# A two-layer latent model on one core: cross attentions that loop over two tiles, shorter prologues, and core attention's weights made during the experts

## The chip, the cores and the metric

One core of a Trainium2 chip. The metric is the device time of one execution in microseconds (us), lower is better. TensorE (PE) has two clock levels, 1.2 and 2.4 GHz; the profile gives the granted clock as a share of the higher one.

## The reference, cut to what matters

64 batches of 32 rows with 256 columns go through two layers of three parts each, and each part adds its result to X (residual):

```
x0  cross attention, 16 heads of 128, 4 key groups, context 64 x 257 x 256 (layer 0)
a0  attention over 512 learned keys and values
e0  router, top 2 of 8 experts, plus one shared expert (inter 128)
c1  "core" attention over the rows themselves: LN, quantised to 8-bit floats per
    linear, heads layer-normed, softmax over 32 rows
x1  cross attention as above with 8 key groups, LN and quantisation (layer 1)
a1  difference attention, f1 feed-forward with Walsh-Hadamard rotations
```

In x0 and x1 a query is projected from the normed row, normalised per head and scored against 257 keys:

```
q = norm(LN(x) Wq) ;  k = norm(ctx Wk) ;  p = softmax(q k^T / sqrt(128))
x = x + (p (ctx Wv)) Wo
```

In c1 and x1 the heads are layer-normed, so the kernel subtracts from the weights of each head their mean over its 128 columns ("centring") before it projects, and in c1 it splits each weight into an upper part in a rounded matmul format and the rest, so that two fast matmuls stand for one exact one; Wo is split into three bf16 parts.

## The kernel before

X is held in SBUF as 16 tiles of 128 rows (four batches of 32). The parts run one after the other, each in a block of its own with its own semaphores, and each engine's program is written out by hand as one stream in order; there is no planner. Between parts GpSimd clears the semaphores.

**Cross attention** (`cross_attention`, both layers; names with `x_` in the rows). `run` (L271) calls `tile(i, cur, prev, nxt)` on each of PE, ACT, DVE and GpSimd: tile 0, then a hardware loop `Fori(1, 15)` of one tile per iteration (its branch instructions are L276 in the rows), then tile 15 and the rest of tile 15's output. SP has such a loop too. A tile has four slots, one for each batch. In a slot PE projects keys from the context (L383), sums squares (L391), scores (L402), transposes probabilities (L412), weighs the context with them (L420) and applies Wv (L429); at its place in the last slots the output Wo (L449) of the tile before, and the query of the tile after: LN'd rows `x_xn` transposed (L358), projected with `x_wq` (L367), transposed back per head (L374). LN of tile i+1 is made on DVE and ACT during tile i: `token_stats` (DVE L803, L806) and `rsqrt_tokens` (ACT L590, L593) at the start of slot 0, the norm itself `x_xn` (DVE L811) somewhat later in slot 0, and PE's L358 waits for it. `copy_weighed` (DVE L919) copies out the weighed context, `round_heads` (DVE L962) quantises in x1. The context of each batch, both ways round, is loaded by SP while the batch before is worked on.

**What stands ahead of the loops.** For x0 the program first has a block in which SP loads all of X (2 MB, L2843) and the identity (L2844) and waits for both; only then does x0's block begin, with SP issuing `x_wq` (2 MB, L288), `x_wk`, the small weights (norm weights, key bias, query bias of 1 MB, mask) and then contexts. PE and DVE wait for the small weights, DVE makes constants (L798, L799), then LN of tile 0, then the query of tile 0 (L367), then keys. In x1 DVE first centres all of `x_wq` (sum L786, subtract L788) and `x_wk`, makes constants (L789 to L795), and only then makes LN of tile 0 (L803 on).

**Experts** (`experts`, names `e_`): 4 passes of four tiles (512 rows as matmul columns). A pass transposes the normed rows (PE L1166), has the router (PE L1522) and its choice on DVE (L1597 to L1617), and nine expert steps: hidden A and B (L1530), gate on DVE (L1623), output Y (L1542), adds to X on DVE (L1586; the ninth, L1588). LN of the next pass (DVE L1141, L1146, L1151, ACT L1159) stands after the last gate. ACT, DVE and PE loop over passes 0 to 2.

**Core attention** (`core_attention`, names `c_`): its prologue loads constants, the three groups of weights and, when their buffer is free, the two halves of Wo; DVE makes 10 constants one after the other, LN of tile 0, centres the head weights (L2143, L2146, L2150), and with ACT splits head weights (L1977, L2154), values (L1934, L1937, L2158) and Wo (L1943, L1945, L2164, L2166). PE transposes tile 0 (L1783), waits for the split head weights before its first projection (L1797), and after the projections of tile 0 waits for the last part of Wo (`late`).

Of the kernel before, what the change touches and what calls it, by code (L numbers as in the profile page):

```python
# [16 lines left out]
P = 128  # L17
# [80 lines left out]
def cross_attention(nc, d, X, Yc, ident, layer, tiles):  # L98
# [25 lines left out]
    with Part(nc) as ctx:  # L124
# [18 lines left out]
        if L1:  # L143
            vecs = sb("vecs", [P, 24])
            inv_in = sb("inv_in", [P, HC])
            smooth = sb("smooth", [P, NH])
            inv_sm = sb("inv_sm", [P, NH])
            qbias = sb("qbias", [P, 1])
            wmean = sb("wmean", [P, HC, NH])
            yscale = sb("yscale", [P, 1])  # L150
# [51 lines left out]
        weights = ctx.semaphore(n + "weights")  # L202
        key_weights = ctx.semaphore(n + "key_weights")
# [83 lines left out]
        def _(sp):  # L287
            sp.dma_start(wq[:], d["wq"].rearrange("(c p) n -> p c n", p=P)).then_inc(weights, 16)  # L288
            if L1:
                loads = [(vecs, d["vecs"]), (smooth, d["smooth"])]  # L290
            else:
                loads = [(bkv, d["bkv"]), (nw, d["nw"]), (bq, d["bq"]), (mask, d["mask"])]
                sp.dma_start(wk[:], d["wk"].rearrange("(c p) n -> p c n", p=P)).then_inc(key_weights, 16)
            for dst, src in loads:
                sp.dma_start(dst[:], src).then_inc(weights, 16)
            if L1:
                sp.dma_start(wk[:], d["wk"].rearrange("(c p) n -> p c n", p=P)).then_inc(key_weights, 16)
# [38 lines left out]
            load_context(0, 0)  # L336
            sp.dma_start(wv[:], d["wv"].rearrange("(c p) n -> p c n", p=P)).then_inc(late_weights, 16)
# [4 lines left out]
            with sp.Fori(1, tiles - 1) as i:  # L342
                tile(i, False, True)
            tile(tiles - 1, False, False)

        NLOADS = 3 if L1 else 5

        @block.tensor
        def _(pe):
            for s in (xt_done, q_done, qt_done, k_done, ss_done, s_done, pt_done, pc_done, v_done, y_done):  # L350
                s.prime(pe)
            pe.wait_ge(weights, 16 * NLOADS)
            pe.wait_ge(ready, 1)
# [211 lines left out]
            for k in range(4):  # L565
                if k >= 2:
                    pe.wait_ge(q_in.sem, q_in.now(0, k - 1))
                project_query(0, k)
# [7 lines left out]
            pe.wait_ge(key_weights, 16)  # L576
# [3 lines left out]
        def _(act):  # L580
# [99 lines left out]
            def slot(i, s, cur, prev, nxt):  # L680
                for t, b in back(i, s, 1, cur, prev):
                    norm_probs(t, b, 3)
                if s == 0 and nxt:
                    rsqrt_tokens(i + 1)
# [30 lines left out]
                if cur:  # L715
# [4 lines left out]
                    norm_probs(i, s, 2)  # L720

# [10 lines left out]
            for k in range(4):  # L732
                copy_query(0, k)
            run(act, tile)

        @block.gpsimd
        def _(pool):
            qT_ready.prime(pool)
            pool.wait_ge(ready, 1)
# [20 lines left out]
        def _(dve):  # L760
# [18 lines left out]
            if L1:  # L779

                for w, nh in ((wq, NH), (wk, G)):
                    if w is wk:
                        dve.wait_ge(key_weights, 16)
                    wr = w[:].rearrange("p c (h e) -> p (c h) e", e=HD)
                    mean = wmean[:].rearrange("p c h -> p (c h)")[:, 0:HC * nh]
                    then(dve.tensor_reduce(mean, wr, AX.X, ALU.add))  # L786
                    then(dve.tensor_scalar(mean, mean, 1.0 / HD, None, ALU.mult))
                    then(dve.tensor_tensor(wr, wr, mean.unsqueeze(2).to_broadcast([P, HC * nh, HD]), ALU.subtract))  # L788
# [5 lines left out]
                for g in range(G):  # L794
                    then(dve.tensor_copy(kT[:, g, SE:KW], vecs[:, 9:10]))  # L795
            else:

                then(dve.scalar_tensor_tensor(qscale[:], nw[:, 0:1], SCALE, nw[:, 1:2], ALU.mult, ALU.mult))  # L798
                then(dve.tensor_scalar(mask[:], mask[:], -1.0, None, ALU.mult))  # L799
            dve.sem_inc(ready, 1)  # L800

# [198 lines left out]
            def slot(i, s, cur, prev, nxt):  # L1000
                if s == 0 and nxt:
                    token_stats(i + 1)
# [75 lines left out]
                if L1:  # L1078
                    for t, p in pair_at(i, s, cur, prev):
                        round_heads(t, p)  # L1080
                for t, b in back(i, s, 1, cur, prev):
# [11 lines left out]
            for k in range(4):  # L1093
                copy_queries(0, k)
            for k in range(4):
                sum_queries(0, k)
            for k in range(4):
                norm_queries(0, k)
            run(dve, tile)
# [5 lines left out]
class TokenNorm:  # L1105
# [33 lines left out]
    def vector(self, dve, i):  # L1139
        for t in range(self.pt):  # L1140
# [6 lines left out]
        a.then_inc(self.aggregated.sem, 1)  # L1147
        dve.wait_ge(self.scaled.sem, self.scaled.now(i, 1))
# [301 lines left out]
def experts(nc, d, X, ident, tiles):  # L1450
# [6 lines left out]
    with Part(nc) as ctx:  # L1457
# [25 lines left out]
        gT = sb("gT", [P, 2, N])  # L1483
        Ab = [bank("A0"), bank("A1")]
# [18 lines left out]
        def _(sp):  # L1503
            for dst, src in ((w1, d["w1"].rearrange("(c p) n -> p c n", p=P)),
# [4 lines left out]
            sp.dma_start(w2[:], d["w2"].rearrange("(e p) n -> p e n", p=P)).then_inc(late_weights, 16)  # L1509

# [36 lines left out]
        def _(act):  # L1547
# [3 lines left out]
            def one_pass(i, nxt):  # L1551
# [8 lines left out]
                if nxt:  # L1560
                    ln.scalar_rsqrt(act, i + 1)

            ln.scalar_rsqrt(act, 0)
            with act.Fori(0, passes - 1) as i:
                one_pass(i, True)
            one_pass(passes - 1, False)

        @block.vector
        def _(dve):
# [21 lines left out]
            def one_pass(i, nxt):  # L1591
# [26 lines left out]
                for e in range(ALL + 1):  # L1618
# [6 lines left out]
                    if e == ALL and nxt:  # L1625
                        ln.vector(dve, i + 1)
# [5 lines left out]
            with dve.Fori(0, passes - 1) as i:  # L1632
                one_pass(i, True)
            one_pass(passes - 1, False)

def core_attention(nc, d, X, Yc, ident, tiles):
# [11 lines left out]
    with Part(nc) as ctx:  # L1649
# [6 lines left out]
        wqk = [sb("wqk_upper", [P, HC, NK * HD], F32R), sb("wqk_lower", [P, HC, NK * HD], F32R)]  # L1656
        wv = [sb("wv_upper", [P, HC, G * HD], F32R), sb("wv_lower", [P, HC, G * HD], F32R)]
        wo = [sb(f"wo_part{j}", [P, NH, H], BF16) for j in range(3)]
        raw = sb("raw", [P, NH // 2, H])
        vecs = sb("vecs", [P, 20])  # L1660
        smooth = sb("smooth", [P, NH])
        inv_in = sb("inv_in", [P, KINDS * HC])
        lnw = sb("lnw", [P, KINDS * HC])
        lnb = sb("lnb", [P, KINDS * HC])
        row_scale = sb("row_scale", [P, KINDS * HC])
        inv_sm = sb("inv_sm", [P, NH])
        qw = sb("qw", [P, 2])
        yscale = sb("yscale", [P, 1])
        wmean = sb("wmean", [P, HC * NK])
# [25 lines left out]
        weights = ctx.semaphore(n + "weights")  # L1695
        head_weights = [ctx.semaphore(f"{n}head_weights{c}") for c in range(HC)]
        value_weights = ctx.semaphore(n + "value_weights")
        late_weights = ctx.semaphore(n + "late_weights")
        ready = ctx.semaphore(n + "constants_ready")
        setup = ctx.semaphore(n + "setup_steps")  # L1700
        centred = ctx.semaphore(n + "head_weights_centred")
        upper = ctx.semaphore(n + "head_weights_upper")
        halves = ctx.semaphore(n + "head_weights_split")
# [1235 lines left out]
```

## Time and profile before

| | |
|---|---|
| median of 3 runs | 3858.22 us (3853.76 to 3859.87) |
| profiled execution, own time | 3862.28 us |
| its span, first to last instruction | 3860.5 us |
| mean granted clock of PE | 0.962 |
| PE / DVE / ACT busy | 90% / 60% / 48% |
| x0, a0, e0 | about 0 to 1130, 1130 to 1377, 1377 to 1622 us |
| c1, x1, a1 and f1 | 1622 to 2079, 2079 to 3505, 3505 to 3860 us |

Times in the rows are from the start of the span. PE is the engine that is nearly always busy, so the table says to look first for the stretches in which it isn't. A row of the timeline reads: start, duration, engine, line, operation, what it writes and reads, and in brackets the idle time before it and what released it.

### The profile page before, as it was taken

The page shows a single profiled execution, that of the slowest core. Times are in us where ns is not written, and L with a number is a line of the kernel's source. Part 1 is how long each engine was busy: PE and PEld are TensorE (multiplying, and loading weights), DVE is VectorE, ACT ScalarE, POOL GpSimd, SP SyncE. Part 2 cuts the span into 40 slices and gives each one's busy share as a digit, 9 for nine tenths or more (in the row PEclk, how much of TensorE's full clock was granted, in tenths as well). Part 3 has the DMA queues.
Part 4 walks back from the last instruction along what each step waited for, and adds up shares of the span by engine and source line. Part 5 has one row for each costly group of instructions (what it writes and reads, how often), then busy time and mean ns, then how long its engine had stood idle before and what let it go on. Part 6 is the DMA issues. An engine that isn't in the chain of part 4 may idle for free. (4 is left out here: it accounts for less than half of the span.)

```text
span 3860.5 us, 75839 instructions
## 1 busy us (share of the span) xinstructions
PE 3479.5 (90%) x25760; PEld 2299.1 (60%) x25760; DVE 2309.8 (60%) x5619; ACT 1860.5 (48%) x5125; POOL 78.0 (2%) x132
## 2 busy tenths in 40 slices
PE   6999999999979989748884899999999999996799
PEld 3666666666643345436663566666666666665555
DVE  3555555555541134578885677777777777766831
ACT  4656565565636631156552544444444444443421
POOL 0000000000000000000000000000000000000000
PEclk9999999999989988879997999999999999998899
DMA  3111111111110010100002011111111111111000
GB/s 122 50 49 49 41 49 49 49 49 41 49 55 1 1 37 0 44 23 0 0 0 88 28 34 41 38 36 39 34 41 33 41 33 41 33 31 50 1 7 15
DMA packets 111903, 137.29 MB, mean 36 GB/s; under 512 B 11200, under 2 KB 90688, under 8 KB 110656
## 3 DMA queue, kind: packets, MB, share of 16 engines
q1 hardware_dynamic: 111808, 136.04, 11.2%
q8 instruction: 57, 0.93, 0.1%
q14 instruction: 38, 0.31, 0.0%
HBM read 133.65 MB, written 2.36 MB: 35 GB/s over the span
## 5 line engine op out<-in xcount | busy, mean ns | idle before, releaser
L383 PE MATMUL x_Kb<-x_cT,x_wk 128*128 128x257 f32 x3072 | 764.7, 384 | 12.9 <-ACT x_sq L631 9.7
L383 PEld LDWEIGHTS x_Kb<-x_cT,x_wk 128*128 128x128 f32 x3072 | 553.0, 190 | 183.3 <-issue 93.6
L420 PE MATMUL x_PC<-x_pT,x_cn 128*128 128x512 f32 x1024 | 474.3, 606 | 4.2 <-DVE x_pT L905 0.8
L651 ACT ACTIVATE x_pr<-x_pr,x_ntop 128x257 f32<-128x257 f32 x512 | 260.9, 510 | 310.4 <-DVE x_ntop L885 167.9
L631 ACT ACTIVATE x_sq<-x_Kb 128x257 f32<-128x257 f32 x512 | 195.6, 382 | 298.6 <-DVE x_kT L868 294.5
L420 PEld LDWEIGHTS x_PC<-x_pT,x_cn 128*128 128x128 f32 x1024 | 184.8, 190 | 244.1 <-issue 242.1
L868 DVE TENSOR_SCALAR x_kT<-x_Kb,x_vecs 128x257 f32<-128x257 f32 x512 | 244.3, 483 | 93.8 <-PE x_Kb L383 88.7
L402 PE MATMUL x_Sb<-x_kT,x_qT 128*32 128x257 f32 (+1 forms) x4096 | 276.5, 384 | 5.0 <-DVE x_pr L888 3.4
L657 ACT ACTIVATE x_pr<-x_pr,x_rps 128x257 f32<-128x257 f32 x512 | 239.3, 499 | 71.0 <-DVE x_rps L898 70.9
L905 DVE COPY x_pT<-x_PTb 128x512 f32<-128x512 f32 x256 | 176.6, 690 | 118.6 <-PE x_PTb L412 116.5
L367 PE MATMUL x_PC<-x_wq,x_xnT 128*128 128x512 f32 x512 | 243.4, 610 | 4.4 <-DVE x_xnT L842 3.9
L449 PE MATMUL x_PC<-x_wo,x_oT 128*128 128x256 f32 x1024 | 235.5, 384 | 6.1 <-DVE x_oT L972 5.3
L919 DVE SCALAR_TENSOR_TENSOR x_pcT<-x_last,x_cT,x_PC 128x512 f32<-128x512 f32 x256 | 190.3, 744 | 75.5 <-PE x_PC L420 72.5
L449 PEld LDWEIGHTS x_PC<-x_wo,x_oT 128*128 128x128 f32 x1024 | 193.9, 192 | 38.5 <-issue 6.2
L880 DVE CUSTOM_DVE_ANT_0 x_pr<-x_Sb,x_rs 128x257 f32<-128x257 f32 x256 | 108.4, 423 | 156.8 <-ACT x_rs L646 149.0
L402 PEld LDWEIGHTS x_Sb<-x_kT,x_qT 128*32 128x32 f32 x4096 | 126.3, 110 | 117.6 <-issue 46.2
L635 ACT ACTIVATE x_kT<-x_Kb,x_bkv 128x257 f32<-128x257 f32 x256 | 121.9, 476 | 112.2 <-PE x_Kb L383 102.2
L644 ACT ACTIVATE x_rs<-x_SSb,x_eps_h 128x257 f32<-128x257 f32 x192 | 91.1, 474 | 175.1 <-PE x_SSb L391 175.0
L1797 PE MATMUL c_B<-c_wqk_upper,c_xq 128*128 128x512 f32 x192 | 89.0, 464 | 77.3 <-DVE c_wqk_lower L2154 26.2
L367 PEld LDWEIGHTS x_PC<-x_wq,x_xnT 128*128 128x128 f32 x512 | 96.4, 193 | 103.0 <-issue 94.3
L412 PE MATMUL x_PTb<-ident,x_pr 128*128 128x128 f32 x1024 | 153.3, 272 | 2.6 <-DVE x_pT L905 2.6
L391 PE MATMUL x_SSb<-x_sq,x_ones 128*32 128x257 f32 x1536 | 123.1, 392 | 32.3 <-ACT x_sq L631 30.0
(301 smaller groups left out, 5694.7 us busy)
## 6 DMA issues: line engine op xcount, KB each, us to landing
x_cT<-in_ctxT SPq DMA_DIRECT2D x128, 257.0 KB, 2.8
x_cn<-in_ctx SPq DMA_DIRECT2D x128, 256.0 KB, 3.0
x_last<-x_last_row SPq DMA_DIRECT2D x128, 256.0 KB, 3.8
x_wq<-in_x_wq SPq DMA_DIRECT2D x2, 2048.0 KB, 7.6
x_wo<-in_x_wo SPq DMA_DIRECT2D x2, 2048.0 KB, 15.7
e_w<-in_e_w SPq DMA_DIRECT2D x3, 1152.0 KB, 7.7
X<-in_x SPq DMA_DIRECT2D x1, 2048.0 KB, 8.2
x_last_row<-x_last_rows SPq DMA_DIRECT2D x128, 2.0 KB
```

The lines of the kernel that those rows point to most:

```text
L367: m = pe.matmul(QB[k][:, :], xnT[:, c, :], wq[:, c, k * 512:(k + 1) * 512], start=c == 0, stop=c == HC - 1)
L383: m = pe.matmul(Kb[j % 2][:, 0:SE], wk[:, c, g * HD:(g + 1) * HD], cT[:, b, c, :], start=c == 0, stop=c == HC - 1)
L402: m = pe.matmul(Sb[v % 2][a * S:(a + 1) * S, 0:KW], qT[:, b, J * g + j, :], kT[:, g, :], start=True, stop=True)
L412: m = pe.transpose(PTb[:, at * P:(at + 1) * P], pr[:, 2 * p + v, c * P:(c + 1) * P], ident[:])
L420: m = pe.matmul(PC[h][:, :], cn[:, b, c, h * P:(h + 1) * P], pT[:, c, :], start=c == 0, stop=c == KC - 1)
L449: m = pe.matmul(PC[1][:, 0:H], oT[:, h, :], wo[:, h, :], start=h == 0, stop=h == NH - 1)
L631: act.activation(sq[:, g, :], Kb[j % 2][:, 0:SE], ACT.Square).then_inc(k_sq.sem, 1)
L651: act.activation(pr[:, v, :], pr[:, v, :], ACT.Exp, bias=ntop[:, u:u + 1], scale=1.0 if L1 else -1.0, accum_out=ps[:, u:u + 1]).then_inc(e ...
L657: act.activation(pr[:, v, :], pr[:, v, :], ACT.Copy, scale=rps[:, u:u + 1]).then_inc(pn_done.sem, 1)
L868: dve.tensor_scalar(kT[:, g, 0:SE], Kb[j % 2][:, 0:SE], vecs[:, 8:9], None, ALU.mult).then_inc(k_raw.sem, 1)
L905: dve.tensor_copy(pT[:, :, 2 * p * P:2 * (p + 1) * P].rearrange("k c (v r) -> k v c r", v=2), PTb[:, :].rearrange("k (v c r) -> k v c r", ...
L919: dve.scalar_tensor_tensor(pcT[:, h, b % NPC, :], last[:, b % 2, :], cT[:, b, h, LAST:SE], PC[h][:, :], ALU.mult, ALU.add).then_inc(pc_cop ...
```

## The change

1. x0's first block is gone. x0's own SP stream issues tile 0 of X (128 KB) and the identity first, then the small weights, `x_wq`, the query bias, `x_wk`, the first context, and then the other 15 tiles of X. PE waits for the first two and for `x_wq`; DVE waits for the rest of X before the statistics of tile 1.
2. `run` loops over two tiles: six iterations of tiles (1,2) to (11,12), then tile 13, 14, 15 written out. SP: seven iterations of two tiles.
3. Statistics and reciprocal root of LN move from slot 0 of tile i (for tile i+1) to slot 3 (for tile i+2), on DVE between `round_heads` and `copy_weighed`.
4. x1: constants and LN of tile 0 come first; `x_wq` is centred in four chunks of 512 columns, each released to PE by itself; the key weights' means are taken on DVE, and GpSimd subtracts them.
5. `CoreWeights`: core attention's weights are loaded, centred and split while the experts run, one small piece of work per expert step on DVE and ACT; their loops over passes are written out. The core attention's prologue has none of it left, and neither has it the wait for Wo.
6. Experts' LN of the next pass: moments at step 4, root at step 5, norm at step 7, not after the last gate.

```diff
-            tile(0, True, False, True)
-            with eng.Fori(1, tiles - 1) as i:
-                tile(i, True, True, True)
-            tile(tiles - 1, True, True, False)
-            tile(tiles, False, True, False)
+            tile(0, True, False, 2)
+            with eng.Fori(0, (tiles - 3) // 2) as j:
+                tile(j * 2 + 1, True, True, 2)
+                tile(j * 2 + 2, True, True, 2)
+            if tiles % 2 == 0:
+                tile(tiles - 3, True, True, 2)
+            tile(tiles - 2, True, True, 1)
+            tile(tiles - 1, True, True, 0)
+            tile(tiles, False, True, 0)
...
+            if not L1:
+                x_rows, ident_src, loaded, tokens_loaded = begin
+                sp.dma_start(X[:, 0:1, :], x_rows[:, 0:1, :]).then_inc(loaded, 16)
+                sp.dma_start(ident[:], ident_src).then_inc(loaded, 16)
...
             load_context(0, 0)
+            if not L1:
+                sp.dma_start(X[:, 1:tiles, :], x_rows[:, 1:tiles, :]).then_inc(tokens_loaded, 16)
...
             def slot(i, s, cur, prev, nxt):
-                if s == 0 and nxt:
-                    token_stats(i + 1)
...
                         round_heads(t, p)
+                if s == 3 and nxt == 2:
+                    token_stats(i + 2)
                 for t, b in back(i, s, 1, cur, prev):
                     copy_weighed(t, b, 0)
...
+            def centre_queries(k):
+                w = wq[:, :, k * 512:(k + 1) * 512].rearrange("p c (h e) -> p c h e", e=HD)
+                mean = wmean[:, :, 4 * k:4 * k + 4]
+                then(dve.tensor_reduce(mean, w, AX.X, ALU.add))
+                then(dve.tensor_scalar(mean, mean, 1.0 / HD, None, ALU.mult))
+                dve.tensor_tensor(w, w, mean.unsqueeze(3).to_broadcast([P, HC, 4, HD]), ALU.subtract
+                                  ).then_inc(queries_centred, 1)
...
+                centre_queries(0)
+                for k in range(1, 4):
+                    centre_queries(k)
+                    copy_queries(0, k - 1)
+                key_weight_means()
...
+    def scalar(self, act, s):
+        c, q = s // 9, s % 9
+        if c < HC and q in (2, 4, 6):
+            self.upper_group(act, c, q // 2 - 1)
...
+                    if e < ALL:
+                        core.vector(dve, i * ALL + e)
+                    if e == 4 and nxt:
+                        ln.vector_moments(dve, i + 1)
+                    if e == 7 and nxt:
+                        ln.vector_norm(dve, i + 1)
...
-            pe.wait_ge(ready, 1)
             transpose_tokens(0)
-            pe.wait_ge(halves, HC)
-            run(pe, tile, lambda: pe.wait_ge(o_rest, 4))
+            run(pe, tile)
```

## Rows read from the trace of the kernel before

**Rows 1.** The page, busy time: us, share of the span, instructions

```profile
PE 3479.5 (90%) x25760; PEld 2299.1 (60%) x25760; DVE 2309.8 (60%) x5619; ACT 1860.5 (48%) x5125; POOL 78.0 (2%) x132
```

**Rows 2.** Windows of a period: busy PE, PEld, DVE, ACT, POOL; clock, DMA

```profile
177.77:244.72 66.95, 66.08 (x418) 43.78 (x419) 37.95 (x104) 40.09 (x105) 2.59 (x4) 1.00 0.15 47
2209.38:2294.22 84.84, 81.99 (x515) 56.78 (x515) 61.25 (x159) 40.99 (x111) 2.29 (x4) 1.00 0.13 38
```

**Rows 3.** Waits of PE, 60 to 1070 us: total, times, longest

```profile
PE x_PC L358 <- DVE x_xn L811: 7.8, 14, 0.7
```

**Rows 4.** Waits of PE, 2150 to 3400 us

```profile
PE x_PC L358 <- DVE x_xn L811: 10.0, 14, 0.7
```

**Rows 5.** Timeline around x_xn in x0, DVE and PE

```profile
174.79 0.42 DVE L803 BATCH_NORM_STATS2 x_stats<-X 128x6 f32 x1
...
177.34 0.37 DVE L811 TENSOR_SCALAR x_xn<-X,x_mv,x_lr 128x256 f32 x1
...
177.77 0.33 PE L358 MATMUL x_PC<-ident,x_xn 128*128 128x128 f32 x1 [0.55 <-DVE x_xn L811]
```

**Rows 6.** Source line of the loops: ns min/median/max, first, last start

```profile
L276 PEldq COMPARE_BRANCH  x28: 76/212/239, 171.3 to 3390.4; - x28
...
L276 DVEq COMPARE_BRANCH  x28: 50/56/68, 174.2 to 3393.0; - x28
```

**Rows 7.** DMA queues, 45 to 190 us: packets, MB, share

```profile
q8 instruction: 6, 0.10, 0.3%
q14 instruction: 7, 0.06, 0.1%
```

**Rows 8.** DMA queues, 190 to 1035 us, the only queue listed

```profile
q1 hardware_dynamic: 35400, 39.49, 15.6%
```

**Rows 9.** Small DMAs in c1's and a1's prologues: KB, us to landing

```profile
c_vecs<-in_c_vecs SPq DMA_DIRECT2D x1, 10.0 KB, 1.6
...
a_subw<-in_a_subw SPq DMA_DIRECT2D x1, 0.5 KB, 3.9
```

**Rows 10.** Timeline and DMA issues of x0's start

```profile
9.61 0.37 SPq L288 DMA_DIRECT2D x_wq<-in_x_wq  x1
...
21.63 0.16 DVE L798 SCALAR_TENSOR_TENSOR x_qscale<-x_nw 128x1 f32<-128x1 f32 x1 [10.25 <-DMA x_mask<-in_x_mask]
...
25.47 1.19 PE L367 MATMUL x_PC<-x_wq,x_xnT 128*128 128x512 f32 x1 [0.56 <-ACT x_xnT L601]
...
x_wq<-in_x_wq SPq DMA_DIRECT2D x1, 2048.0 KB, 7.6
```

**Rows 11.** Timeline of PE and windows at a pass boundary of the experts

```profile
1503.96 1.97 PE L1166 MATMUL e_T<-ident,e_xn 128*128 128x128 f32 x8 [5.25 <-DVE e_xn L1151]
...
1510.05 3.76 PE L1530 MATMUL e_A<-e_xnT,e_w 128*128 128x512 f32 x4
...
1504.00:1517.00 13.00, 12.31 (x33) 7.84 (x34) 5.52 (x32) 3.31 (x5) 0.00 (x0) 0.53 0.00 0
1517.00:1561.00 44.00, 42.76 (x136) 25.46 (x134) 20.61 (x45) 6.06 (x9) 0.00 (x0) 1.00 0.00 0
```

**Rows 12.** Timeline of PE and one DVE group, core attention's prologue

```profile
1631.32 0.66 PE L1783 MATMUL c_B<-ident,c_xn 128*128 128x128 f32 x2 [12.02 <-DVE c_xn L2006]
1658.14 0.79 PE L1797 MATMUL c_B<-c_wqk_upper,c_xq 128*128 128x512 f32 x1 [26.17 <-DVE c_wqk_lower L2154]
...
1698.12 0.79 PE L1797 MATMUL c_B<-c_wqk_upper,c_xq 128*128 128x512 f32 x1 [23.33 <-DVE c_wo_part L2166]
...
L2154 DVE TENSOR_TENSOR c_wqk_lower<-c_qk,c_wqk_upper 128x3072 fp32r<-128x3072 f32 x1 | 3.3, 3349 | 0.0
```

**Rows 13.** Timeline of PE and DVE, x1's prologue

```profile
2107.24 0.66 PE L358 MATMUL x_PC<-ident,x_xn 128*128 128x128 f32 x2 [31.71 <-DVE x_xn L811]
...
2088.59 4.42 DVE L786 TENSOR_REDUCE x_wmean<-x_wq 128x32 f32<-128x4096 f32 x1 [6.47 <-DMA x_smooth<-in_x_smooth]
...
2121.47 0.75 DVE L850 TENSOR_SCALAR x_qn<-x_PC,x_vecs 128x512 f32<-128x512 f32 x1 [0.96 <-PE x_PC L367]
```

More of the change, by code:

```diff
@@ L351, in _ @@
                 s.prime(pe)
-            pe.wait_ge(weights, 16 * NLOADS)
-            pe.wait_ge(ready, 1)
+            if not L1:
+                pe.wait_ge(begin[2], 16 * 2)
             def transpose_tokens(t):
@@ L1098, in _ @@
                 norm_queries(0, k)
+            if not L1:
+                dve.wait_ge(begin[3], 16)
+            token_stats(1)
             run(dve, tile)
@@ L1452, in experts @@
+def experts(nc, d, X, ident, tiles, core):
     n = "e0_"
@@ L1483, in experts @@
         gT = sb("gT", [P, 2, N])
+        core.stage(ctx)
         Ab = [bank("A0"), bank("A1")]
@@ L1509, in _ @@
             sp.dma_start(w2[:], d["w2"].rearrange("(e p) n -> p e n", p=P)).then_inc(late_weights, 16)
+            core.load(sp)
         @block.tensor
@@ L1559, in one_pass @@
                     act.activation(g1[:, e % 2, :], Ab[e % 2][:, :], ACT.Silu).then_inc(h_silu.sem, 1)
-                if nxt:
-                    ln.scalar_rsqrt(act, i + 1)
+                    core.scalar(act, i * ALL + e)
+                    if e == 5 and nxt:
+                        ln.scalar_rsqrt(act, i + 1)
             ln.scalar_rsqrt(act, 0)
-            with act.Fori(0, passes - 1) as i:
-                one_pass(i, True)
-            one_pass(passes - 1, False)
+            for i in range(passes):
+                one_pass(i, i + 1 < passes)
         @block.vector
@@ L1654, in sig @@
             return Signal(ctx, nc, n + name, per, unit)
[L1656 to L1669, printed above, removed]
+        wqk, wv, wo, vecs, qw, yscale = core.wqk, core.wv, core.wo, core.vecs, core.qw, core.yscale
+        lnw, lnb, inv_sm = core.lnw, core.lnb, core.inv_sm
         eps = sb("eps", [P, 1])
@@ L1761, in core_attention, with run @@
         OB = banks[4:8]
-        def run(eng, tile, late=None):
+        def run(eng, tile):
             tile(-1, None, False, True, True)
-            if late:
-                late()
             tile(0, None, True, True, True)
@@ L1974, in _ @@
             rsqrt_tokens(0)
-            for c in range(HC):
-                act.wait_ge(centred, c + 1)
-                act.activation(wqk[0][:, c, :], STAGE[c][:].rearrange("p h e -> p (h e)"), ACT.Copy).then_inc(upper, 1)
-            split_values()
-            run(act, tile, split_out)
+            run(act, tile)
         @block.vector
@@ L1987, in _ @@
             dve.memset(eps_ln[:], 1e-10)
-            dve.wait_ge(weights, 16 * 2)
-            step = [0]
-            def then(ins):
-                step[0] += 1
-                ins.then_inc(setup, 1)
-                dve.wait_ge(setup, step[0])
+            dve.sem_inc(ready, 1)
             def token_stats(t):
```

345 lines of the change are left out of this document (216 added, 129 removed).

## The prediction, on record before the changed kernel was run

> **What bounds the kernel now.** I read the busy times on the page first: PE works 90% of the span [rows 1], so time can only come from the rest, and I looked for where that lies. The windows of one period of each cross attention's loop answer for two thirds of the span: in x0 a tile takes 66.95 us with PE busy 66.08, in x1 84.84 us with PE busy 81.99, both at full clock [rows 2]. There is next to nothing to win inside: PE's waits over x0's loop have one repeated entry, x_xn from DVE, 0.55 us a tile, and x1 has the same one at 0.7 [rows 3 to 5]. The large idle times stand at the seams: PE starts its first projection at 25.47 in x0 [rows 10]; at each of three pass boundaries of the experts it idles 5.25 us and then works 13 us at clock 0.53, that is at the lower level, 1.2 GHz [rows 11]; core attention's prologue holds idle times of 12.02, 26.17 and 23.33 us [rows 12]; x1's holds 31.71 [rows 13]. These are what parts 1, 4, 5 and 6 of the change touch. The chain that ended last goes through all of them, so I take each in its own stage.
>
> **Start of x0 (part 1).** Now wq is issued at 9.61, behind a block that waits for 2 MB of X, and DVE's wait for the small weights, which share the queues with wq and the 1 MB query bias, ends at 21.63; the projection starts 3.84 us after that [rows 10]. Changed, five small transfers go ahead of wq, each some 0.5 us to issue, so wq is issued at about 3.2. It takes 7.6 us for its 2 MB [rows 10] and lands at about 10.8. LN of tile 0 needs only 128 KB and the small weights and is done in that shadow. The projection then starts at about 10.6 to 11, so 14.9 us earlier. What is late next: the query bias (1 MB at wq's rate, +3.8 us: 14.6), the first copy of queries waits for that, not before 13 in any case; the rest of X lands near 22 and is needed when DVE has normed the queries, about 26. I take 15, between 12 (bias and X collide with contexts) and 16.
>
> **Experts (parts 5 and 6).** At a boundary the moments, the root and the norm of the next pass lie between the last gate and PE's transposes; moved ahead by several steps they lie in DVE's idle time, which is 23.4 of 44 us [rows 11], and the wait of 5.25 us goes. If PE doesn't pause, its clock need not fall either: 13 us at 0.53 hold 6.1 us of lost clock. That is 11.3 a boundary; the router's own short waits remain, I take 10, and for three boundaries 30. Core's work comes on top of DVE: of the pieces the largest now seen whole is 3.35 us (3072 columns, twice) [rows 12]; cut in three, a piece is 1.1 to 2.3 us. One expert step is 44/8.5 = 5.2 us with 2.4 DVE busy [rows 11], so 2.8 are free, and a piece fits. Where it doesn't, the gate of the next step is late and PE waits a few tenths: over 33 steps at 0.3 that is 10 us, the lower bound for this part is therefore 18 or so. Two DMA issues ahead of the experts' weights cost 0.8. ACT has 6.06 busy of 44 [rows 11] and room for its share; its silu waits behind a piece of at most 1.3 us. Pass 0 has LN and 10 constants of core in the shadow of the weights' load.
>
> **Core attention's start (part 5).** Constants and the load before them go from ahead of LN: transposes move from 1631.32 to about 1626.7. Then only the rounding of the two transposed halves (about 5.5 us from the transposes to the last of it) stands before the first projection: about 1632.2 in place of 1658.14, so 25.9 us [rows 12]. The wait for Wo, 23.33 us, goes [rows 12]; the next tile's rounded rows are ready 0.8 us after PE comes there, so 22.5. After that wait PE runs some 5.6 us at the lower clock, which gives back about 2. Together 50 (48 to 54).
>
> **Start of x1 (part 4).** DVE starts at 2088.59, when wq has landed, with a reduction of 4.42 us, as long a subtraction, and half of both for the keys; LN comes 16 us later, PE's transposes at 2107.24, and the last copy of queries ends at 2122.2 [rows 13]. Changed, constants and LN are done while wq comes, about 2090.7. A chunk is a quarter of the two long ones plus gaps, 2.6 us. Four chunks, three copies of 0.75 us, key means and the eight small copies, then the last copy: 2090.7 + 10.4 + 2.3 + 2.6 + 1.6 + 0.75 = 2108.4 to 2109.2 where now 2122.2 stands: 13 (9 to 16, the low end if PE at the lower clock is what the copies wait for). GpSimd's subtraction of the key means has no row: between DVE's 2.3 us for the same and several times that it would be done before 2118, when the first key is wanted. The Trainium skill, page "GPSIMD Engine Reference", section 3.1, gives 4497 ns for an add of 2048 columns there against 2293 on DVE; the trace's DVE row for half of a 4096-column operation (2.2) agrees with the second, and by either the sum stays.
>
> **Statistics two tiles ahead (part 3).** It reads as if it took the 0.55 us from PE's wait for x_xn. But DVE works without a gap from before L803 (174.79) until x_xn (177.34) [rows 5], and the new place of the two instructions is one L919 earlier in that same run of work. x_xn stands behind the same sum of durations. I take 0; bounded by nothing below and by both waits whole above, 7.8 + 10.0 = 18 [rows 3, 4].
>
> **The loop over two tiles (part 2).** A loop's edge costs nothing now: the branch takes 212 ns on PE and 56 ns on DVE [rows 6], PE's sequencer is some 3 us ahead of its work, and DVE's gap lies inside the same busy run. Fewer edges save nothing. What can cost is the code. PE fetches six blocks of 16 KB and the others seven of 8 KB between 45 and 190 us, two tiles of the program [rows 7]; then, over twelve iterations, not one [rows 8]: one tile's program stays with each engine. Two tiles are twice as much: 837 matmuls and loads become 1674 in x0 on PE, about 1030 become 2060 in x1, and DVE's 104 and 159 become 208 and 318, each with its waits beside it [rows 2]. The trace of before holds no loop of that size. If it doesn't stay, each taken edge must fetch its first block, and nobody can fetch it ahead; DVE, whose sequencer is only about 0.6 us ahead of its work, and which is busy without a gap up to x_xn, hands all of it on to PE. A fetch from memory is nearest to a small DMA: 1.6 to 3.9 us from issue to landing [rows 9], less 0.35 for the gap there already: 1.3 to 3.5, I take 2.4. Ten taken edges give 24, 13 to 35; if only x1's five, 12. I hold it likely for x1 and open for x0, so 20.
>
> The Trainium skill, page "Runtime: NRT & Kernel Launch", section "Instruction fetch mechanics", says that most engines hold 32 KiB of instructions and PE 128 KiB (512 and 2048 instructions), filled as a FIFO in sequence, and that a taken branch to a target outside it waits for a DMA fetch. Rows 8 agree that a tile's program stays. By the rule x1's PE (over 2060) and DVE overflow for certain and x0's DVE perhaps; the sum by it is the 12 to 24 above, without it 0.
>
> **Sum.** Gains 15 + 30 + 50 + 13 = 108, fetches 20 against it: 88. The profiled execution took 3862.3 by its own time, so 3774; the median of the runs shown is 4.1 lower, at 3858.2, which leads to 3770.
>
> **Rivals.** (a) The doubled loops stay resident. For it: fetching that ends after one iteration shows a good margin for what was needed until now; against it: twice the size. Time 3858 - 108 = 3750. (b) Statistics ahead do save the wait: x_xn's place in DVE's order might be reached sooner if ACT's root (0.48 us of ACT ahead of key copies) was the real wait. Time up to 18 less, 3752 with fetches. Against it is the gapless run in the timeline. (c) Core's pieces on DVE and ACT make the experts' steps late: three loads of ACT's tables where LN's root sits between silus, a piece behind which the gate waits. At 0.6 us for each of 33 steps 20 us are lost: 3790. (d) The clock falls at the experts' boundaries anyway, since the router's 16 short matmuls come there: 3 x 6.1 = 18 less gained, 3788. (e) The other side: fetches. They would have to cost 108/10 = 10.8 us for each edge before the kernel is slower, if every engine fetched its blocks one after the other with nothing ahead. A block on PE holds work for some 18 us (66.95 us over 3.6 blocks), far more than 3.9, so streaming is hidden. If each of an edge's blocks on DVE cost 2.4 and there were 5 or more of them, 12 us an edge would give 3870. (f) The change does not do what it says at a seam, because a transfer lands late (x0: contexts behind X, core: heads' second load): 10 to 15 lost, 3783.
>
> **How the numbers follow.** Forecast as above, gains with some fetches: 0.52, own range 3760 to 3780. (a) 0.16, (b) 0.05, (c) 0.09, (d) 0.09, (e) 0.02, (f) 0.07. The predicted time is 3770. The range 3742 to 3794 takes in (a), (c), (d) and the ends of the fetches (13 to 35) but not (e) or two mishaps together. What a measurement of this kernel can tell from no change is 0.2%, 8 us. Faster 0.96: every case but (e) and a part of several added; same 0.02, slower 0.02.
>
> **What would show it.** Right: x0's first L367 near 10.6; core's first L1797 about 8 us after its block's start and no idle time of over 3 us before PE in its first tile; x1's first key 13 us nearer to its block's start; experts' boundaries without the 5 us and with clock near 1; packets of the instruction queues at every second tile of x1, PE's wait for x_xn longer in each such tile by 1.3 to 3.5 and unchanged at 0.55 in the others. Wrong: no such packets (a); that wait gone everywhere (b); PE waiting on the gate L1623 or on silu in many steps (c); a clock of 0.5 behind each boundary (d); a stage that is longer than now outside of these places.

## The result, and the profile after

The changed kernel took 3795.36 us in the median of 4 runs (3786.47 to 3803.35), the kernel before 3859.05 beside it; the ratio is 0.9836, 95% interval [0.9808, 0.9863]. In five more runs, on another chip, it took 3797.25 (3792.49 to 3800.08), ratio 0.9838 [0.9824, 0.9852]. So 64 us were gained (61 in the five more runs) where 88 were forecast, and the time lies 1.4 us above the stated range. It is faster, as forecast; the size was wrong.

The page of the changed kernel: busy times, and the queues that fetch instructions.

```profile
PE 3474.9 (92%) x25760; PEld 2295.8 (61%) x25760; DVE 2310.1 (61%) x5644; ACT 1869.2 (49%) x5135; POOL 81.3 (2%) x133
...
q8 instruction: 180, 2.95, 0.3%
q14 instruction: 169, 1.38, 0.1%
```

PE's work is the same [rows 1]; the instruction fetches are 349 packets, where the page of the kernel before has 95. Queue q8 brings PE's instructions in packets of 16 KB, q14 those of the other engines in packets of 8 KB: in the runs below, PE's doubled loop by itself has packets on q8 alone, DVE's or ACT's on q14 alone. Over the loop of layer 0, 190 to 1000 us, where before there was no such packet [rows 8], these queues are now:

```profile
q8 instruction: 52, 0.85, 0.4%
q14 instruction: 54, 0.44, 0.2%
```

Source line of the loops (nanoseconds min/median/max, first and last start), against [rows 6]:

```profile
L282 PEldq COMPARE_BRANCH  x12: 83/3546/3777, 222.2 to 3146.2; - x12
...
L282 DVEq COMPARE_BRANCH  x12: 60/68/68, 225.9 to 3150.5; - x12
```

The ten branches that jump back take PE's sequencer about 3.5 us, where they took 0.21. On DVE the branch itself stays short (68 ns where it was 56), but what comes behind it is late. The timeline at the first such edge of layer 0:

```profile
225.85 0.75 DVE L951 SCALAR_TENSOR_TENSOR x_pcT<-x_last,x_cT,x_PC 128x512 f32<-128x512 f32 x1
...
226.15 1.13 PE L399 MATMUL x_Kb<-x_cT,x_wk 128*128 128x257 f32 x4 [0.16 <-issue]
...
229.27 0.16 DVE L930 RECIPROCAL x_rps<-x_ps 128x1 f32<-128x1 f32 x1 [2.67 <-issue]
...
229.49 0.51 ACT L678 ACTIVATE x_pr<-x_pr,x_rps 128x257 f32<-128x257 f32 x1 [2.95 <-DVE x_rps L930]
...
231.11 0.37 DVE L843 TENSOR_SCALAR x_xn<-X,x_mv,x_lr 128x256 f32 x1
...
231.54 0.44 PE L374 MATMUL x_PC<-ident,x_xn 128*128 128x128 f32 x2 [2.95 <-DVE x_xn L843]
```

PE's own 3.6 us leave it only 0.16 us short, because its sequencer was that far ahead; DVE sits 2.67 us for "issue", that is for nothing that the profile shows, and PE's wait for x_xn grows from 0.55 [rows 5] to 2.95. The windows of two tiles one after the other, the first with an edge in it and the second without, against [rows 2]:

```profile
161.77:231.54 69.77, 66.34 (x419) 43.70 (x419) 38.16 (x104) 40.31 (x104) 2.57 (x4) 1.00 0.16 48
231.54:298.48 66.94, 66.08 (x419) 43.80 (x419) 38.00 (x104) 39.75 (x103) 2.57 (x4) 1.00 0.15 48
```

The other stages. Timeline of PE at x0's start, at the experts' start and second boundary, at the core attention's first projection, and at x1's start:

```profile
11.16 9.25 PE L383 MATMUL x_PC<-x_wq,x_xnT 128*128 128x512 f32 x16 [2.99 <-DMA x_wq<-in_x_wq]
...
29.71 2.00 PE L399 MATMUL x_Kb<-x_cT,x_wk 128*128 128x257 f32 x8 [0.78 <-ACT x_qTn L645]
...
1379.08 1.21 PE L1766 MATMUL e_T<-e_wr,e_xnT 128*128 128x8 f32 x5 [2.41 <-DMA e_places<-in_e_places]
...
1484.00 1.09 PE L1218 MATMUL e_T<-ident,e_xn 128*128 128x128 f32 x8
1485.88 1.95 PE L1766 MATMUL e_T<-e_wr,e_xnT 128*128 128x8 f32 x16 [0.80 <-ACT e_xnT L1225]
1487.69 1.96 PE L1774 MATMUL e_A<-e_xnT,e_w 128*128 128x512 f32 x4
...
1600.60 0.79 PE L2002 MATMUL c_B<-c_wqk_upper,c_xq 128*128 128x512 f32 x1 [4.87 <-DVE c_xq L2205]
...
2004.99 0.69 PE L374 MATMUL x_PC<-ident,x_xn 128*128 128x128 f32 x2 [10.22 <-DVE x_xn L843]
2012.22 5.40 PE L383 MATMUL x_PC<-x_wq,x_xnT 128*128 128x512 f32 x8 [6.54 <-DVE x_wq L825]
...
2031.42 1.08 PE L390 MATMUL x_PC<-ident,x_qn 128*128 128x128 f32 x4 [6.79 <-DVE x_qn L893]
```

The 5.25 us ahead of the experts' transposes are gone, and at this boundary, the second, hidden A takes 1.96 us where it took 3.76 at the lower clock [rows 11]. The router of pass 0, though, waits 2.41 us for its weights; in the kernel before it was

```profile
1386.16 3.55 PE L1522 MATMUL e_T<-e_wr,e_xnT 128*128 128x8 f32 x16 [0.83 <-DMA e_places<-in_e_places]
```

Core attention's 26.17 is 4.87 and its 23.33 is gone [rows 12]. x1's 31.71 [rows 13] has become 10.22, but 6.54 and 6.79 stand behind it.

The changed kernel's profiled run was the shortest of its four. The second profile, of a run of 3800 us, is nearer to the median, so I took the account by stages from that one, as differences between the starts of the same PE instructions in it and in the kernel before:

```
stage                                        forecast   measured
x0, start to its first key                     -15        -14.7
x0 and x1, tiles 3 to 13 (ten edges)           +20        +34.0  (17.9 + 16.1)
experts, first to last transposes and end      -30        -22.1  (2.4, 8.5, 10.6, 0.6)
core attention                                 -50        -50.0
x1, end of core attention to x1's third tile   -13         -9.3
all else                                         0         -0.4
sum                                            -88        -62.5
```

### The profile page after: what moved, and what is told of

Its sections match the earlier page's. It is cut to its first block and busy times, and to the rows that moved or that the text cites. A ratio compares the mean times of both kernels' runs of the same rounds, so it can differ in the third digit from the quotient of the medians.

```text
span 3784.7 us, 74777 instructions
## 1 busy us (share of the span) xinstructions
PE 3474.9 (92%) x25760; PEld 2295.8 (61%) x25760; DVE 2310.1 (61%) x5644; ACT 1869.2 (49%) x5135; POOL 81.3 (2%) x133
## 3 DMA queue, kind: packets, MB, share of 16 engines
q8 instruction: 180, 2.95, 0.3%
## 5 line engine op out<-in xcount | busy, mean ns | idle before, releaser
L399 PE MATMUL x_Kb<-x_cT,x_wk 128*128 128x257 f32 x3072 | 773.9, 387 | 13.1 <-ACT x_sq L652 8.0
L428 PEld LDWEIGHTS x_PTb<-ident,x_pr 128*128 128x128 f32 x1024 | 128.4, 141 | 36.1 <-issue 9.4
```

The costliest lines, as they stand in the source:

```text
L399: m = pe.matmul(Kb[j % 2][:, 0:SE], wk[:, c, g * HD:(g + 1) * HD], cT[:, b, c, :], start=c == 0, stop=c == HC - 1)
L428: m = pe.transpose(PTb[:, at * P:(at + 1) * P], pr[:, 2 * p + v, c * P:(c + 1) * P], ident[:])
```

## The experiments

The edits of the loop below start from the changed kernel unless said otherwise; from "The statistics back where they were" on they start from the one-tile kernel, which is the first of them, and the last two from the written-out one. Times are medians; a ratio is to the kernel before on the same chip.

**One tile per iteration, and none of the rest undone.**

```diff
-            with eng.Fori(0, (tiles - 3) // 2) as j:
-                tile(j * 2 + 1, True, True, 2)
-                tile(j * 2 + 2, True, True, 2)
-            if tiles % 2 == 0:
-                tile(tiles - 3, True, True, 2)
+            with eng.Fori(1, tiles - 2) as i:
+                tile(i, True, True, 2)
```

> The changed kernel with one tile per iteration in both cross attentions' loops and all else as it is. Theory A (every taken edge of the doubled loops waits for its instructions): the ten longer tiles of the trace, 5 x 2.8 and 5 x 3.1 us, go, no instruction packets inside the loops, 3757 for a profiled run at best and about 3762 to 3765 in the median, spread no wider than 9 us. Rival B (the longer tiles come from the statistics two tiles ahead, which stay): no change, 3790 to 3795.

3761.31 (3758.56 to 3762.84), ratio 0.9748 [0.9735, 0.9761]. All tiles take 66.94 and 84.76 us, and there is no instruction packet in the loops. Against the changed kernel on the same chip the doubled loops cost 36 us. The spread is 4 us.

> The changed kernel itself, to know its spread and to have it beside the others on one chip. Theory A (its spread comes from the clock, which falls behind some of the pauses at the loops' edges): 3786 to 3804 again, wider than the 8 us of the kernel before, the long runs with the lower mean granted clock. Theory B (those four runs were chance): as narrow as the kernel before, near 3790.

3797.25, range 7.6 us, so not wider than the kernel before (13 us on that chip). Theory A of the wide spread fell; but the profile does show the lower clock at edges. Three tiles of layer 0 in it; the second holds an edge, the first and third hold none, but stand behind one and have a stretch at half clock:

```profile
232.55:302.50 69.95, 68.93 (x418) 46.07 (x418) 38.02 (x104) 39.72 (x103) 2.57 (x4) 0.96 0.15 46
302.50:372.01 69.51, 66.17 (x418) 43.73 (x419) 38.18 (x104) 40.27 (x104) 2.57 (x4) 1.00 0.16 48
372.01:440.54 68.53, 67.51 (x419) 44.91 (x419) 38.01 (x104) 39.74 (x103) 2.57 (x4) 0.98 0.16 47
```

So an edge costs 2.3 to 2.9 us as a pause, and some edges 1.2 to 3 more in the tile behind them, in PE work that runs slower.

**The doubled loops alone, on the kernel before.**

> The kernel before with the loops over two tiles and nothing else of the change. Theory A (the edges alone): ten edges at 2.8 us and now and then a fallen clock, 3887 to 3895. Rival B (the stall needs something else of the change): 3859.

3894.20 (3891.71 to 3901.27), ratio 1.0097 [1.0081, 1.0112]: 36 us slower. Nothing else of the change is needed for the stall. PE's waits, 160 to 900 us:

```profile
PE x_PC L365 <- DVE x_xn L818: 22.4, 11, 4.2
```

The total is the same from both sides, but its parts are not, so that is in part a coincidence. Between the same PE instructions of tiles 3 to 13 this kernel is 30.2 us behind the kernel before in layer 0 and 6.2 in layer 1, the changed kernel 17.9 and 16.1 (second profile). Layer 0's waits reach 4.2 us here. In layer 1 (2300 to 3000 us) there are as many packets, yet the wait for x_xn doesn't grow; instead PE waits at the edges for its own sequencer, the second line:

```profile
PE x_PC L365 <- DVE x_xn L818: 4.6, 8, 0.8
PE x_PTb L419 <- issue: 4.5, 4, 1.2
```

What an edge costs thus hangs on what stands behind it in each engine's program; why layer 1 gets off so lightly here stays open.

**Which engine's miss is it.** `run` chooses the loop by engine, and the other engines, SP too, loop over one tile; for instance

```diff
+            if eng.engine != nc.vector.engine:
+                with eng.Fori(1, tiles - 2) as i:
+                    tile(i, True, True, 2)
+            else:
                 with eng.Fori(0, (tiles - 3) // 2) as j:
```

> Only PE loops over two tiles; DVE, ACT, GpSimd and SP over one. PE's branch takes 3.5 us at an edge in the trace of the changed kernel, and its sequencer is about 3.5 us ahead of its work. Theory A (PE's own miss is hidden by that lead, DVE's sets the price): within 3 us of the one-tile kernel, PE's branch still 3.5 us long. Rival B (PE's miss is the price, DVE's only runs beside it): 10 x 2.8 us slower than the one-tile kernel, as the changed kernel.

> Only DVE loops over two tiles. Theory A: all of the price, 25 to 30 us above the one-tile kernel, PE's wait for x_xn 3 us in every second tile. Rival B: none of it. If DVE's body of one layer fits where the other's doesn't, half of it.

> Only ACT loops over two tiles (about 326 instructions in layer 0, 392 in layer 1). In the changed kernel ACT's gap at an edge lies beside DVE's. Theory A (its body stays resident, being about as long as DVE's single one of layer 1): no packets, as the one-tile kernel. Rival B (it misses too): up to 3 us at each edge, 15 to 30 us.

PE alone: 3765.40, ratio 0.9751. DVE alone: 3790.65, 0.9813 [0.9796, 0.9829]. ACT alone: 3784.93, 0.9800 [0.9784, 0.9817]. The one-tile kernel's ratio is 0.9748, so that is nothing, 25 us and 20 us. PE's waits for x_xn, 160 to 900 us, in these three in that order, and between them PE's branch in the first:

```profile
PE x_PC L375 <- DVE x_xn L844: 6.2, 12, 0.6
```

```profile
L286 PEldq COMPARE_BRANCH  x12: 83/3456/3842, 222.9 to 3121.6; - x12
```

```profile
PE x_PC L375 <- DVE x_xn L844: 18.3, 11, 3.1
```

```profile
PE x_PC L375 <- DVE x_xn L844: 14.7, 11, 2.4
```

PE pays 3.5 us in its sequencer at every edge and loses next to nothing by it: in its profile tiles 3 to 13 are 0.6 us longer in layer 0 and 1.4 in layer 1 than in the kernel before, where PE sits up to 0.7 us for "issue" at an edge. In the same measure DVE alone costs 29.0 us and ACT alone 21.4, and the changed kernel 29.8 in its first profile and 34.0 in its second. So DVE's miss is most of the price, and the engines' prices don't add up (25 and 20 against 36 in the medians): stalls of two engines at one edge lie partly beside each other. My theory A for ACT fell: its doubled loop of 319 traced instructions misses, though DVE's of 333 stays. DMA between 240 and 850 us, ACT alone doubled:

```profile
q14 instruction: 21, 0.17, 0.1%
```

```profile
L282 PEldq COMPARE_BRANCH  x12: 87/242/402, 221.9 to 3115.8; - x12
```

One thing I had not expected: in layer 0 (1810 traced instructions on PE, 404 on DVE, 319 on ACT) there is no instruction packet between 240 and 850 us; in layer 1 (2244 and 651 on PE and DVE) they go on, 66 between 2300 and 3000 us, and are hidden. So layer 0's doubled loops do fit. The changed kernel has 82 and 92 packets in these two windows. I read it so that without the hint the fetching runs on past the loop's end and pushes out its head; no run looked into the memory itself.

**No loop.** Tiles 1 to 13 written out.

> The changed kernel with tiles 1 to 13 of both cross attentions written out, no loop at all. All of it must be fetched, but in sequence. Theory A (only the taken branch to a place that is not there costs, streaming is hidden): as the one-tile loop, within 2 us of it, with some 200 more packets of the PE instruction queue. Rival B (any fetching of code costs, through DMA or because the stream can't keep up): between the one-tile loop and the changed kernel, or slower than both.

3751.94 (3749.22 to 3755.69), ratio 0.9724 [0.9710, 0.9738]: 9 us below the one-tile kernel, which neither theory had. Fetching in sequence is hidden (268 instruction packets in all). A tile takes 66.59 us instead of 66.94 and 84.55 instead of 84.76. That is not the edge: in the changed kernel tiles without an edge take 66.94 as well (the second window above). The written-out code has no register arithmetic for the semaphore waits; DVE's tile in layer 0 holds 159 traced instructions instead of 206. DVE is not where the gain lies, though: PE's wait for x_xn is 0.52 us a tile instead of 0.55. In layer 0 the 0.35 us stand at three places, ahead of the first matmul that weighs the context (0.15, 0.11 and 0.10 us): there PE idles 50 to 70 ns in the loop, with such arithmetic in its sequencer (32 ns each) just before, and written out it doesn't idle. That fits the arithmetic on PE as the cause, which no run changed by itself; layer 1's 0.2 us were not traced to a place. 13 x 0.35 + 13 x 0.2 = 7 us of the 9 are in these tiles.

**The statistics back where they were.**

```diff
             def slot(i, s, cur, prev, nxt):
+                if s == 0 and nxt:
+                    token_stats(i + 1)
...
-                if s == 3 and nxt == 2:
-                    token_stats(i + 2)
```

ACT's root of LN goes back with them.

> The one-tile kernel with the statistics and the root back where they were, at the start of slot 0 for the next tile. Theory A (the move is worth nothing, since x_xn stands behind the same DVE work either way): as the one-tile kernel within 4 us, PE's wait for x_xn 0.55 us a tile in both. Rival B (the move saves something, or costs): more than 0.3 us a tile, so over 8 us.

3826.29 (3825.19 to 3827.17), ratio 0.9913 [0.9899, 0.9926]: 64 us slower than the one-tile kernel by the ratios. That is neither A nor a price of the move that I could have argued. Layer 0 is unchanged (66.95 us a tile), all of it lies in layer 1: 89 to 91 us a tile. Its waits of PE and its instruction queue over eight tiles there:

```profile
PE x_PC L368 <- DVE x_xn L836: 34.6, 8, 4.5
```

```profile
q14 instruction: 40, 0.33, 0.2%
```

Five packets a tile and a stall at every edge, by a one-tile loop of 331 traced instructions on DVE, which in the kernel before has the same 331 and has no packet. What differs is where the code lies. Nor can the statistics' place be it, since the kernel before has them there too.

**Placing the head of DVE's loop.** A fetch block is what one packet of the instruction queue brings, and a slot is the place of an instruction in it. The loop's first instruction is put at a given slot, in both layers.

```diff
-            with eng.Fori(1, tiles - 2) as i:
+            if eng.engine == nc.vector.engine:
+                with nc.Fori(1, tiles - 2, engines=..., head_slot={eng.engine: 0}) as i:
```

> The kernel with one-tile loops and the statistics one tile ahead, with the head of DVE's loop placed at slot 0 of a fetch block in both layers; no other change. Theory A (DVE's 331 instructions stay only where they touch three blocks of 128, not four): the stalls of layer 1 go, 65 us, so within 4 us of the one-tile kernel (3761). Rival B (the later statistics themselves make layer 1's DVE late): 3826 as before.

> The one-tile kernel with the head of DVE's loop at slot 96 of a fetch block in both layers. Theory A: layer 1's 333 instructions then touch four blocks and every one of its 12 taken edges stalls, 4.8 us a tile with the clock's falls, 50 to 65 us slower than the one-tile kernel; layer 0's 206 touch three and stay. Rival B (place doesn't matter, the length alone does): 3761.

The slow kernel with its head at slot 0: 3768.30 (3764.22 to 3770.70), ratio 0.9762 [0.9749, 0.9775], 58 us back. The fast kernel with its head at slot 96: 3804.04 (3800.76 to 3807.61), ratio 0.9854 [0.9839, 0.9869], about 41 us lost, all in layer 1 (87 to 89 us a tile; layer 0 keeps 66.95). Waits over the same eight tiles, the first and the second:

```profile
PE x_PC L372 <- DVE x_xn L840: 5.7, 8, 0.7
```

```profile
PE x_PC L372 <- DVE x_xn L841: 24.7, 8, 3.3
```

At slot 0 q14 has no packet over the eight tiles, at slot 96 it has 40. This settles it for DVE: the place decides whether a loop of 331 to 333 stays; both directions were run. Other slots, and the place of ACT's or of the doubled loops, were not. And with the stall out of the way the move of the statistics is worth 0.07 us a tile in layer 1 (84.83 against 84.76) and nothing in layer 0. The medians differ by 0.14%, which their intervals don't separate; in the profile the kernel with its head at slot 0 is 9 us behind when x0's tile 3 begins, before the steady part of the loop. Where an edge does stall, the kernel with the statistics behind it has the longer wait, 34.6 us over eight tiles against 24.7; since the two heads also lie at different places, that the statistics make it longer is argued.

**Experts' LN back behind the last gate.**

> The one-tile kernel with the experts' moments, root and norm of the next pass back behind the last gate; core attention's pieces stay in the steps. Theory A (at each of three boundaries 5.25 us of idle and the clock after it come back): 3 x 8 to 10, so 24 to 30 us slower than the one-tile kernel. Rival B (most of the experts' gain came from elsewhere, the clock falls there anyway): 3 x 5.25, 16 us slower or less.

3783.30 (3778.43 to 3789.00), ratio 0.9801 [0.9788, 0.9815]: 21 us slower by the ratios, under the range of A. From transposes to transposes it is 5.0, 8.1 and 10.4 us in the profile, and 0.6 from the last ones to the end. The second of them again has the wait and the lower clock:

```profile
1490.91 1.97 PE L1212 MATMUL e_T<-ident,e_xn 128*128 128x128 f32 x8 [5.13 <-DVE e_xn L1197]
...
1497.00 3.76 PE L1768 MATMUL e_A<-e_xnT,e_w 128*128 128x512 f32 x4
```

**Core's constants loaded behind the experts' weights.**

> The one-tile kernel with the two small loads of core attention's constants issued behind the experts' weights and not ahead of them. The router of pass 0 now idles 2.41 us for the last of its weights. Theory A: 1 to 2 us gained, which is less than a run can tell; to be seen in the trace as that wait down to about 1.4. Rival B: DVE's constants come later and push the first steps, which costs it again.

3756.19 (3753.24 to 3759.60), ratio 0.9730 [0.9717, 0.9743]. The router's wait of pass 0:

```profile
1371.43 3.55 PE L1760 MATMUL e_T<-e_wr,e_xnT 128*128 128x8 f32 x16 [1.40 <-DMA e_places<-in_e_places]
```

In the one-tile kernel's profile it is 2.95, so it is 1.5 us shorter, and 1.0 more comes back with 3.4 us less at half clock in pass 0. The 2.6 us together lie under what a run can tell. DVE's constants hurt nothing.

**All that helped, together.**

> The changed kernel with tiles 1 to 13 written out, core's constants loaded behind the experts' weights, and x1's eight small key copies put ahead of the quantising of tile 0, where DVE waits. Expected from the written-out kernel (3752): 1.5 us by the load, 1.5 by the copies: 3749, and below the kernel before by 109.

> The written-out kernel with core's constants loaded behind the experts' weights, without the moved key copies. Expected: 3752 less 1.5 to 5: 3747 to 3750. Rival: what the earlier load gives is taken back by where the clock falls later, 3752 to 3755, as in the version with the copies moved too.

3754.62 (3753.93 to 3756.01), ratio 0.9727 [0.9713, 0.9740], and 3753.62 (3746.89 to 3756.92), ratio 0.9723 [0.9709, 0.9736]. Neither is measurably below the written-out kernel alone. In the first of them x1's first key comes 0.9 us sooner after core attention than in the one-tile kernel, and the stretch from there to its third tile takes 1.7 us more, with 3.4 us more at the lower clock: what is gained is given back where the clock falls next. The three written-out versions are the fastest and can't be told apart; the first is 2.8% below the kernel before and 1.2% below the changed kernel.

## Why the prediction was wrong

**The loop over two tiles is the step that failed, by its size.** The mechanism was forecast and came: packets at every edge, ten stalls, PE waiting longer for x_xn in those tiles alone. It was put at 2.4 us for a likely five and an open five edges, "so 20". All ten stalled, and they cost 34.0 in the second profile and 36 in the medians, 3.5 each. Two things were missed. First, layer 0 was held open, on its length, which took 4 us off the ten pauses; it stalls too, and the hinted loop shows that length wasn't the reason. Second, the pause of PE brings the lower clock behind it at some edges, 10 us at half clock in each layer's loop of the second profile: that is 8 us, which the sum had no term for. The pause itself was sized nearly right, 2.7 us in layer 0 and 2.5 in layer 1 on average, 2 us over the ten. Of the forecast's shortfall of 26 us, 14 are here; by themselves they would have left the time inside the stated range, and it took the two terms below to pass it. That PE's own miss would hide in its lead and DVE's would not was right but for 2 us, and PE alone doubled shows it; that ACT's miss alone costs 20 us had no place in it. And that nobody can fetch the first block of a taken edge ahead holds for the loop as written: with the hint it is fetched in time.

**Experts**: 22.1 in place of 30, 8 of the shortfall. The part numbers of the table run from transposes to transposes, so each holds the idle time ahead of a boundary and the clock behind the boundary before it. The idle 5.25 us went at all three. What failed is that the clock would stay up behind them: it does behind the second (that pass is 10.6 shorter), it is low for 3.4 us behind the first, and behind the third for 6.8 us, where almost nothing is won (0.6). Hidden A there, in the second profile:

```profile
1550.23 3.76 PE L1774 MATMUL e_A<-e_xnT,e_w 128*128 128x512 f32 x4
```

The router's matmuls stand behind all three boundaries alike, so they alone don't bring the clock down. So rival (d) came in part. In pass 0, which the sum gave 0.8 us, the router waits 2.41 us for the last of its weights behind core's two loads, 3.00 in the second profile, where it was 0.83, and PE's clock is then low for 17 us instead of 14. That core's pieces fit into the steps was right: they stay at 5.16 us apiece, and rival (c) did not come.

**x1's start**: 9.3 in place of 13. The first key is 13.2 us nearer to the end of core attention, as summed, but the third tile's transposes only 9.3. From the first key to there the changed kernel takes 4 us more for the same matmuls, at a clock of 0.94; the windows, first of the changed kernel and then of the one before:

```profile
2037.00:2119.00 82.00, 74.53 (x446) 49.45 (x446) 52.20 (x143) 41.72 (x115) 4.57 (x8) 0.94 0.08 23
2131.50:2209.40 77.90, 70.36 (x447) 46.16 (x447) 52.57 (x144) 41.59 (x114) 4.63 (x8) 1.00 0.08 25
```

That the clock is low there because PE paused for the chunks of wq and for x_qn (6.54, 1.81, 1.30 and 6.79 us) is argued from the order of events; no run removed the pauses.

The key means' subtraction on GpSimd took 3.61 us and was hidden.

```profile
2025.68 3.61 POOL L765 TENSOR_TENSOR x_wk<-x_wk,x_kmean 128x2048 f32<-128x2048 f32 x1 [984.30 <-DVE x_kmean L832]
```

The Trainium skill, page "GPSIMD Engine Reference", section 3.1, has 4497 ns for an add of that size; the row, a subtraction of a mean that is repeated over each head, is 0.9 us shorter, and the row decides.

**x0's start and core attention** came as summed, 14.7 for 15 and 50.0 for 50. **The statistics**, at 0, came as forecast too (0.07 us a tile), but only a run with DVE's loop placed could show it.

The Trainium skill, page "Runtime: NRT & Kernel Launch", section "Instruction fetch mechanics", names 512 instructions for most engines, filled in blocks, and has a taken branch wait when its target lies outside the two blocks that are held. The runs agree that a taken branch to what isn't there waits, and that streaming is hidden. The length against the figure of 512, which the prediction took as the test, is not it: 319 on ACT and 331 on DVE miss without hint or placing, 404 on DVE stay with the hint. That the place among the blocks counts goes with the page's blocks; it gives them as 16 KiB, and q14's packets are 8 KB.

## What to carry to other kernels

Before a loop's body is made longer, or code ahead of it moved, look at the instruction queues inside the loop: none means that it is resident, and if packets appear, the price is at the edge, on the engine with the least lead, and PE's clock may add to it. DVE's branch tells the two apart as well, here 56 ns against 68 in most iterations. An edit that moves a loop's head can cost more than the edit is about, so compare tile periods with and without packets before crediting the edit; a hint on the closing branch, a placed head, or no loop at all took the price away here. And a gain at a seam of PE's work must be read past the next stretch at the lower clock, since a pause that is only split up may keep it low.

## What the runs showed of the hardware that I had not expected

- A DVE loop of 331 to 333 traced instructions stays or misses by its place alone: with the head at slot 96 five packets of 8 KB and 3.1 us of PE's wait a tile, with the head at slot 0 no packet and 0.7 us.
- A branch hint not only hid the fetch, it ended it in layer 0: 82 packets between 240 and 850 us without it, none with it.
- PE's branch can take 3.5 us at each of ten edges and cost 2 us in all, while a miss on ACT costs 2 us an edge. With ACT alone doubled, PE's wait for x_xn reaches 2.4 us in layer 0; in layer 1 it doesn't grow, and PE waits up to 1.3 us for ACT's squares of the keys (x_sq) instead.
- Written-out tiles are 0.35 and 0.2 us shorter than looped ones of the same work, with an edge or without; in layer 0 it is PE that idles less.
- The same doubled loops cost 36 us on either kernel, but 30 and 6 us by layer on one and 18 and 16 on the other.
